# A routed mixture-of-experts stage on one core: six full routed tiles taken ahead of the last token steps

## The reference

```
h = patches @ W.T + b                                # 768 -> 192
h = h + attention(layernorm(h))                      # 12 heads of 16, causal over 16 tokens, RoPE
x = layernorm(h);  t = rmsnorm(x) * norm_scale
g = t @ gate_w.T + gate_b                            # 16 experts
top_vals, top_idx = top_k(g, 4);  route_w = softmax(top_vals)
a_e = swiglu(t @ mlp1_w[e].T + mlp1_b[e])            # 192 -> 2*384 -> 384
y_e = a_e @ mlp2_w[e].T + mlp2_b[e]                  # 384 -> 192
h = h + x + sum over the 4 chosen experts of route_w * y_e
```

## Time and profile before

| | us |
|---|---|
| median of 3 runs (495.38 to 497.33) | 496.5 |
| the profiled execution | 492.28 |
| its span, first to last instruction | 490.5 |
| TensorE busy, matmuls | 436.2 (89%) |
| TensorE busy, weight loads | 385.4 (79%) |
| ScalarE busy | 313.7 (64%) |
| VectorE busy | 292.7 (60%) |
| GpSimd busy | 238.7 (49%) |
| mean granted TensorE clock, share of full speed | 0.946 |

### The profile page before, as it was taken

The page is one execution under the profiler, slowest core; times in us unless marked ns, Lnnn a source line. Parts: engine busy times, 40 slices in busy tenths (PEclk is TensorE's granted clock), DMA queues, the critical chain, the costliest instruction groups (busy, mean ns, idle before and its releaser), DMA issues.

```text
span 490.5 us, 14416 instructions
## 1 busy us (share of the span) xinstructions
PE 436.2 (89%) x3877; PEld 385.4 (79%) x3878; DVE 292.7 (60%) x992; ACT 313.7 (64%) x816; POOL 238.7 (49%) x285
## 2 busy tenths in 40 slices
PE   3589999999999666699999999999999999999980
PEld 3366777786776454499999999999999999999970
DVE  0357789888889747055555555555555556555550
ACT  1057877887787732277667776667766677666730
POOL 2113367877777667103336545344454445444453
PEclk9999999999999655699999999999999999999995
DMA  7766457757793112233335434333443444332332
GB/s 223 189 186 175 141 147 217 207 167 208 186 277 106 71 63 104 81 90 62 60 54 77 61 61 70 61 52 57 68 68 59 59 59 68 61 42 27 33 34 24
DMA packets 42106, 49.72 MB, mean 101 GB/s; under 512 B 6387, under 2 KB 33507, under 8 KB 42052
## 3 DMA queue, kind: packets, MB, share of 16 engines
q1 hardware_dynamic: 27604, 34.35, 26.2%
q0 software_dynamic: 14448, 14.72, 19.3%
HBM read 30.82 MB, written 18.23 MB: 100 GB/s over the span
## 4 chain that ended last, share of the span: by engine, by line
PE 66%; DVE 13%; issue 8%; POOL 6%; DMA 3%; SPq 2%; ACT 1%; POOLq 1%; DVEq 0%; ACTq 0%
PE bank L591 23%; PE bank L613 15%; PE bank L599 13%; PE bank L571 4%; POOL routed_rows L1129 3%; PE bank L421 3%; PE bank L437 2%; PE bank L415 2%; PE bank L438 2%; PE bank L460 1%; DMA b_sb<-b 1%; DVE sc L833 1%; DVE stats L885 1%; POOL p_pair L1158 1%; DVE xn L800 1%
## 5 line engine op out<-in xcount | busy, mean ns | idle before, releaser
L1203 POOL DMA_INDIRECT out_rows<-x_sb,row_to x79 | 123.5, 1563 | 162.3 <-DMA out_rows<-x_sb,row_to 76.2
L591 PE MATMUL bank<-rT,w_now 128*128 128x128 f32 x948 | 124.0, 281 | 0.3 <-ACT rT L636 0.3
L591 PEld LDWEIGHTS bank<-rT,w_now 128*128 128x128 f32 x948 | 115.1, 193 | 5.2 <-ACT rT L636 0.5
L722 ACT ACTIVATE k_spread<-bank,w_now 128x128 f32<-128x128 f32 x237 | 70.0, 372 | 59.3 <-PE bank L599 59.3
L636 ACT ACTIVATE w_now<-w_sb 128x1158 f32 x79 | 92.3, 1170 | 18.7 <-issue 13.2
L1068 DVE TENSOR_TENSOR v_sb<-bank,w_now 128x384 f32<-128x384 f32 x79 | 44.0, 557 | 88.8 <-PE bank L599 69.0
L613 PE MATMUL bank<-w_sb,p_spread 128*128 x474 | 83.9, 327 | 0.1
L1129 POOL DMA_INDIRECT routed_rows<-packet,row_i x64 | 64.1, 1001 | 30.4 <-PE bank L481 16.1
L613 PEld LDWEIGHTS bank<-w_sb,p_spread 128*128 128x128 f32 x474 | 76.1, 190 | 0.5 <-issue 0.4
L1081 DVE SCALAR_TENSOR_TENSOR p_spread<-k_spread,v_sb 128x384 f32<-128x384 f32 x79 | 44.1, 559 | 34.4 <-ACT k_spread L722 30.8
L599 PE MATMUL bank<-rT,w_now 64*128 64x128 f32 x948 | 64.3, 282 | 0.0
(11 more groups left out here) (185 smaller groups left out, 582.8 us busy)
## 6 DMA issues: line engine op xcount, KB each, us to landing
x_sb<-patches SPq DMA_DIRECT2D x16, 384.0 KB, 3.5
w_sb<-w SPq DMA_DIRECT2D x32, 192.0 KB
w_sb<-w SPq DMA_DIRECT2D x16, 288.0 KB
w_sb<-w SPq DMA_DIRECT2D x64, 48.0 KB
wtok_sb<-routed_rows SPq DMA_DIRECT2D x25, 106.0 KB, 2.0
routed_rows<-zero_row SPq DMA_DIRECT2D x17, 106.0 KB
out_rows<-h SPq DMA_DIRECT2D x16, 96.0 KB
out_rows<-x_sb,row_to POOLq DMA_INDIRECT x79, 3.5
```

Of the source, the lines that this page charges most:

```text
L591: last = mm(dst[:, c * P:(c + 1) * P], w[:, a:a + P], t[:, part, :], start=(start and c == 0), stop=(not start and c == ICH - 1))
L722: last = nc.scalar.activation(gate_act[b][:, a:a + P], ps_glu[b][:, a:a + P], ACT.Silu, bias=w1_now[b][:, GLU_B + c:GLU_B + c + 1], scale= ...
L1203: G.indirect_dma_start(out=out, out_offset=bass.IndirectOffsetOnAxis(ap=row_to[:, b % NY:b % NY + 1].bitcast(U32), axis=0), in_=y_out[b % ...
```

## The change

From step 16 on, with the rows of token tiles 0 to 9 scattered, the counts of these ten tiles give a first table: six (EARLY) tiles that are full already, from experts 0, 1 and 2. They are routed tiles 0 to 5 of the 79. The final table lists the other 73 (FINAL), from the counts less what the six have taken.

- **Heads.** The heads of experts 0 to 3 are cleared by four indirect DMAs on GpSimd in step 2 (`clear_heads`), which raise the four `added` semaphores by 16 (ADDS_FROM); SyncE clears the other 13.
- **Early table.** Step 16: one more small product on TensorE and 8 instructions on VectorE (`early_counts`). Step 17: 12 instructions (`early_table`), and TensorE turns the table at the end of the step. Step 18: VectorE copies it and scales b1 (`early_done`), which TensorE turns ahead of the projection.
- **Loads.** SyncE loads the rows of tiles 0 to 5 behind the base stores of tiles 8 and 9, once the early table is there.
- **TensorE.** It turns the rows of tiles 0 and 1 at the end of step 18, does the first layer of tile 0 at the end of step 19, that of tile 1 in step 20 behind the bias product. After step 21: turn and first layers of 2 and 3, the final table's products, second layers of 0 and 1, turn and first layers of 4 and 5, second layers of 2 to 5, then the loop from tile 6 on. The WARM products go.
- **ScalarE.** Copies of rows and weights of tiles 0 and 1 in step 19, the table load of Silu and the gate of tile 0 in step 20, the rest behind step 21.
- **VectorE.** The linear halves of 0 and 1 behind step 21 and ahead of the final table; their products behind the table; 2 and 3 behind the copy of the table; then the weighing and 4 and 5.
- **Buffers.** NY = 8 result buffers, the four new ones in the score tiles; the row buffers are listed in another order; some products of the last steps go to other banks.

```diff
+EARLY, EARLY_TILES = 6, 10
+FINAL = SLOTS - EARLY
-        NY = 4
+        NY = 8
@@ SyncE
-            for e in range(EXPERTS + 1):
+            for e in range(ADDS, EXPERTS + 1):
                 sp.dma_start(routed[e * REGION:e * REGION + P, :], zero_row[:]).then_inc(heads_out, 16)
-            with sp.Fori(TILES - 8, TILES) as t:
+            store_base(TILES - 8)
+            store_base(TILES - 7)
+            sp.wait_ge(early_ready, 1)
+            sp.wait_ge(s["embedded"], TILES)
+            for buf in range(PACKETS):
+                sp.wait_ge(scattered[buf], 16 * TOPK * ((EARLY_TILES + PACKETS - 1 - buf) // PACKETS))
+            for j in range(EARLY):
+                load_rows(j, j)
+            with sp.Fori(TILES - 6, TILES) as t:
                 store_base(t)
@@ TensorE, step
+                if n == TILES + 2:
+                    bank_free(("k_spread_ready", TILES))
+                    turn(ps_b1, b1_sb[:], ident[0:2 * ICH * EXPERTS, 0:2 * ICH * EXPERTS]).then_inc(b1_turned, 1)
...
+                if n == TILES + 1:
+                    pe.wait_ge(early_step, EARLY_STEPS)
+                    for i in range(4):
+                        last = mm(ps_etab[:, i * EARLY:(i + 1) * EARLY], of_early[0:EARLY, i:i + 1], ident[0:EARLY, 0:EARLY],
+                                  start=True, stop=True)
+                    last.then_inc(early_turned, 1)
+                if n == TILES + 2:
+                    pe.wait_ge(early_ready, 1)
+                    pe.wait_ge(setup_dve, 5)
+                    pe.wait_ge(experts_in, 16 * LOADS_E * EXPERTS)
+                    turn_early(0)
+                if n == TILES + 3:
+                    bank_free(("place_ready", TILES - 2), ("base_full", TILES - 3))
+                    first_layer(0, 0, True)
+                if n == TILES + 4:
+                    bank_free(("top_i_ready", TILES))
+                    first_layer(1, 1, False)
@@ TensorE, behind the steps
+            turn_early(1)
+            first_early(1)
...
-            for i in range(WARM):
-                mm(banks[0][:, 0:INNER], ident, h0[:, i:i + 2, :].rearrange("p a d -> p (a d)"), start=True, stop=True)
...
+            second_early(0)
+            turn_early(2)
+            first_early(2)
+            second_early(1)
+            second_early(2)
...
+            for j in (EARLY, EARLY + 1):
+                turn_rows(j, j, 16)
@@ ScalarE, step
+                if n == TILES + 3:
+                    act.wait_ge(early_ready, 1)
+                    act.wait_ge(setup_dve, 5)
+                    act.wait_ge(experts_in, 16 * LOADS_E * EXPERTS)
+                    experts = experts_early(0)
+                    turned_early(0)
+                    for j in range(2):
+                        copy_w1(j, j, experts[j])
+                        note_weight(j, j, experts[j])
...
+                if n == TILES + 4:
+                    nc.scalar.activation(spare_w[:], spare_w[:], ACT.Silu)
+                    gate(0, 0)
@@ VectorE, step and behind it
                 at(3, turn_probs)
+                if n == TILES + 1:
+                    early_table()
+                if n == TILES + 2:
+                    early_done()
                 at(4, attn_add)
                 at(4, attn_stats)
+                if n == EARLY_TILES + STAGES - 1:
+                    early_counts()
...
+            for j in range(2):
+                linear(j, j)
             dve.wait_ge(counted, 1)
...
             add_bias(TILES - 1)
+            for j in range(2):
+                product(j, j)
             dve.wait_ge(table_turned, 1)
...
+            for j in (2, 3):
+                linear(j, j)
+                product(j, j)
...
+            for j in (0, 1):
+                weigh(j, j)
+            for j in (4, 5):
+                linear(j, j)
+                product(j, j)
+            for j in range(2, EARLY):
+                weigh(j, j)
@@ GpSimd
+            def clear_heads():
+                pool.wait_ge(setup_dve, 3)
+                alone(pool)
+                for i in range(ADDS):
+                    G.indirect_dma_start(out=routed, out_offset=bass.IndirectOffsetOnAxis(
+                        ap=head_i[:, i:i + 1].bitcast(U32), axis=0),
+                        in_=zero_row[:], in_offset=None).then_inc(added[i], 16)
...
                 if tile(0) is not None:
                     embed_root(tile(0))
+                if n == 2:
+                    clear_heads()
...
+                    pool.wait_ge(added[b % ADDS], ADDS_FROM if isinstance(j, int) and j < ADDS else owed_to(j - ADDS, b))
```

549 lines of the change are left out of this document (333 added, 216 removed).

## The result

The change made the kernel slower by 0.7%: median 499.48 us (496.96 to 501.03, 17 runs) against 495.97 us (493.41 to 498.77, 17 runs), ratio 1.0068 with an interval of 1.0048 to 1.0088. The forecast was 490.2 us, with a range of 485.0 to 495.0. So the fair reading is "nothing gained, up to 0.7% lost", where 1.3% was forecast. Single executions over 1.5% above the fastest of the same kernel are left out of every ratio.

The account below looks back on a forecast made before the run. TensorE was taken to bound the routed loop, with a hole ahead of it behind GpSimd's scatters. Gross 22.0 us less 14.2 lateness left 7.8, less 1.5 tail 6.3: 496.5 to 490.2 us, range 485.0 to 495.0.

Parts of the forecast that it names:

- What is removed: Routed loop six tiles shorter, 20.4 us, and the first pair's half-clock start gone, 1.6 us: gross 22.0 us.
- Step 2: Four cleared heads on GpSimd delay p_pair of tile 0 and VectorE's transpose: shift 2.4 us, bounds 0 and 3.4.
- Steps 16 to 18: Early table's work on VectorE and turning on TensorE add lateness of 1.2, 0.2, 0.4 and 0.4 us.
- Steps 19 to 21: First layers of tiles 0 and 1 fill TensorE's idle time, ending about 196; ScalarE's copies free, GpSimd's scatters off the path.
- The hand-over: From step 21 to tile 6's first layer, at 219.3: lateness 14.2 us, leaving 7.8 us net on TensorE.
- The tail: Last add comes 7.2 us behind the last result, before 5.7: cost 1.5 us, bounds 0 and 3.
- (c): In-order queues hold each other more than followed, 5 us more: saving 0 to 4, about 494.5 us; chance 0.20.
- (d): Clock stays low through all early tiles and into the loop, costing 12 us: slower, 502 us; chance 0.06.
- (b): Step 2's lateness is made up and the clock rises in step 19: saving 8.5 to 12, about 486.5 us; chance 0.24.

Follow-up runs that it names:

- after_fourth: The changed kernel, unaltered, timed and profiled again on chip B beside the kernel before: ratio 0.9995, profile span 491.9 us.
- before_again: The kernel before, unchanged, timed and profiled again on chip B: ratio 1.0015 to itself, profile span 490.8 us.
- before_heads: The kernel before with only the heads of experts 0 to 3 cleared by four GpSimd writes in step 2: ratio 1.0027 to the kernel before.
- Reads and order together: The changed kernel with heads in step 1, register reads ahead of waits, table products between first layers of tiles 2 and 3: ratios 0.9894 and 0.9834 to before.
- the filler products: TensorE products that nobody reads, added to the kernel with heads in step 1, reads ahead and table products between: ratios 0.9819 and 0.9791 to before on chip B.
- the order: The changed kernel with the table's products between the first layers of tiles 2 and 3, not behind both: ratio 0.9976 to before on chip B.
- the reads: The changed kernel with early tiles' register reads on ScalarE and TensorE moved ahead of the waits: ratio 0.9965 to before on chip A.
- the fillers: The changed kernel with only unread TensorE products added in its gaps: ratio 1.0015 to before on chip C.
- before_third: The kernel before, unchanged, timed and profiled again on chip D: ratio 0.9975 to itself, profile span 493.3 us.

## Why the forecast was wrong

By its own steps, in the order of the forecast; sizes from after_fourth against before_again unless named.

- **What is removed.** Right: 22.0 forecast, 22.1 measured, with the loop at 6.80.
- **Step 2.** The mechanism was right in each link, with p_pair at 38.97, VectorE idle 2.28 before its transpose; the bare cost was 2.26 us (before_heads), 2.4 forecast. The term was 3.56 in the changed kernel, whose clock was 0.50 behind the gap. The text took the trace to say that nothing was made up later, which held: the stretch from tile 4 to tile 15 is 103.2, as before. The Trainium skill, "SBUF — State Buffer", in the section "A bandwidth-pool intuition that's wrong", gives some 3.1 us to a GpSimd-issued DMA beside a VectorE copy; four of them, an estimate, would be 12.4 us, which is 7 more than the forecast's 5.3 and not the 8 that it wrote. The four ran 1.21, 0.99, 0.96 and 0.96 us, while VectorE was busy for 2.20 of these 5.05 us and did no copy, so the trace of after shows no such hold, as the earlier trace rows did not.
- **Steps 16 to 18.** 1.8 us forecast up to the values of tile 15, 1.3 measured. Right, if high. The sign, the values product of tile 15 done at about 179.6, came at 179.9 on chip B (start 178.38, and 1.5 us at half clock). Of the 26.36 us of after, 1.4 are the pause, which the forecast didn't know; that it was at half clock over the whole of step 17 is the rest, argued and not shown.
- **Steps 19 to 21.** Cover right: scatters and rows never ended a wait of TensorE from tile 2 on. ScalarE's copies for tiles 0 and 1 were called free, since it idled 4.61 us there; ahead of them stood 1.36 us of register reads, which had been left out. TensorE idled 1.59 us for the copies in after and not at all in after_fourth, where it came late itself, at half clock. The sign "2.4 GHz before 192" came for moments only: 0.92 in 186 to 188 of after, then 0.50 through the first layer of tile 0 and 0.52 through that of tile 1, which took 4.5 us where the forecast had 2.5. In after_fourth it was 0.50 through that of tile 0 and 0.73 through that of tile 1. In after the first layer of tile 1 so ended 20.7 us behind the values product of tile 15, 2.8 later than forecast.
- **The hand-over.** This step failed. 41.2 us forecast, 47.77 measured (48.93 in after): 6.6 us. By the rows of after, counted from the values of tile 15: the final table was ready 1.7 us later than forecast, which cost nothing. The first layers of tiles 2 and 3 started 2.9 us late, which is the lateness of tile 1 above, and took 7.3 us, mostly at half clock, not 4.4, so that the table's products ended 5.7 us late. From there to the end of the second layers of tiles 0 and 1 it took 4.1 us and not 2.8, 0.87 of it register reads, which makes 7.0. To the first layer of tile 6 0.7 are added. In after_fourth the same three places are 1.5, 3.1 and 5.5 us late. So what the forecast had mis-sized is the products from tile 1 on, put down at full clock, and register reads, put down at nothing. It had the order of this queue right (the table's products behind the first layers) and had not asked what that order costs.
- **What the edits there were worth.** Reads and order together (with the heads a step earlier) were worth 3.8 and 6.6 us of the hand-over in the two sets on chip B (46.87 to 43.02, 47.77 to 41.21), the filler products another 3.2 and 2.5 on top. Alone, the order was worth nothing on chip B, the reads 1.5 us by their rows on A, the fillers 0.8 on C, where there are pauses. That they hide one another fits this and is only in part shown.
- **The tail.** Last addition 2.1 us later, 1.5 forecast, within 0 to 3. The gaps are as forecast, 4.33 and 1.86; the row is one of the earlier trace rows's kind:

```profile
482.06 1.55 POOL L1413 DMA_INDIRECT out_rows<-x_sb,row_to  x1 [2.72 <-DVE sc L1135]
483.92 1.55 POOL L1413 DMA_INDIRECT out_rows<-half_s,row_to  x1 [0.30 <-issue]
488.25 1.55 POOL L1413 DMA_INDIRECT out_rows<-sc,row_to  x1 [2.77 <-DMA out_rows<-half_s,row_to]
490.11 1.55 POOL L1413 DMA_INDIRECT out_rows<-sc,row_to  x1 [0.30 <-issue]
```

  with the last weighing at

```profile
481.60 0.41 DVE L1135 TENSOR_SCALAR sc<-bank,row_w 128x192 f32<-128x192 f32 x1
```

- **The reference point.** The first profile of before had a quick start-up, 32.13 us; the changed kernel had 31.98 to 34.83 in its four profiles of the same code. The Trainium skill, "TensorE: Matmul & The Clock Gate", part 1, says that how many products run cold at a start varies from run to run; the traces agree: of one and the same kernel, the first q and k products of token tile 1 took 1.53 us at 26.74 in after and 0.88 us at 25.79 in after_fourth. It is not part of the error: on chip B both start at 32.

Sum on chip B: heads 1.2 too little, steps 16 to 18 0.5 too much, hand-over 6.8 too little (16.8 against 10.0 above before; 0.2 more than the 6.6 above, as the forecast counted from 205.08, where the ledger has the first product of tile 0 at 204.87), tail 0.6 too little, loop 0.1 too little, and 0.6 by which start and token loop were quicker: 1.2 - 0.5 + 6.8 + 0.6 - 0.1 - 0.6 = 7.4 us, from a saving of 6.3 to a loss of 1.1 between the spans. Of the rivals, (c), queues that hold each other, was the right one, together with the mechanism of (d), a clock that stays low through most of the early work; (c) was priced at 5 us more than the forecast and came to 6.8, the low clock in it. Rival (b) fell: the lateness of step 2 wasn't made up, and the clock did not hold at its upper level from step 19 on. That the first comparison came out at 1.0068, where chip B gave 1.000, fits the pauses, which are in its profile of after and not in that of before; it isn't shown, as chip C has pauses too and gave 1.0016. Which chips its 17 runs used is not known.

## What to carry to other kernels

Work moved into a hole is worth what the new order of every in-order queue leaves of it: write that order down with register reads and waits as entries, and ask of each entry behind a wait whether it could stand ahead. Try such edits together too, as each alone may show little where two others still hold the same point. An idle engine is cover only for work that is ready to run in it. Filler products paid here only together with the other edits; whether the removed waits or the chip made the difference is open. And put a number on every product at the clock that the rows around it show, not at the one that you hope for.

## What the runs showed of the hardware that was not expected

- A register read from a table is 0.30 us on TensorE's queue (median of 79 in after) and 0.28 on ScalarE's (median of 8), with its range check 0.5 to 0.7; two tiles' worth behind a wait were 1.36 us of idle ScalarE, the first one on TensorE 0.87.
- After a wait of 2.53 us in dense work, the granted clock of after was 0.50 (window 43 to 46) and 0.94 in the next 3 us; behind a like wait of 2.51 us in before_heads it stayed at 1.00. It was 0.50 all through 166 to 176 in after, with 7.6 us of TensorE work, and all through 178.4 to 190 in after_fourth, with 10.7 of 11.6.
- On three of four chips VectorE paused for 1.2 to 3.8 us where nothing in the profile released it, and a run of 23 small instructions that takes 2.5 us took 9.1 in before_third. The cause is open.
- The same kernel before had medians of 493.1 to 499.7 us on the four chips, 1.3%, more than the effect of most edits here, so only comparisons within one set of runs on one chip were of use.
